# One of sixteen one-hot comparisons per group moved from VectorE to GpSimd

## The reference, cut to what matters

```python
x = _layernorm(x + _L0_gnn_ref(x, edge_index, ...))   # GIN: S = segment_sum(X[src], dst), 4 times
x = _layernorm(x + _L1_gnn_ref(x, edge_attr_64, edge_index, ...))   # edge MLP
x = _layernorm(x + _L2_gnn_ref(x, edge_index, ...))   # segment softmax, 3 times
x = _layernorm(x + _L3_gnn_ref(x, edge_attr_20, src, dst, edge_weight, ...))   # filtered interaction
```

## Time and profile before

| what | value |
|---|---|
| median of three runs | 2368.28 us |
| the profiled execution | 2367.29 us |
| span of the profiled execution, first to last instruction | 2365.6 us |
| mean granted TensorE clock | 0.788 of full speed |
| `adjacency`, first to last instruction | about 103.8 to 302.4 us of the span |
| of these, VectorE without a gap | 107 to 295 us |

### The profile page before, as it was taken

The page is one execution under the profiler, slowest core; times in us unless marked ns, Lnnn a source line. Parts: engine busy times, 40 slices in busy tenths (PEclk is TensorE's granted clock), DMA queues, the critical chain, the costliest instruction groups (busy, mean ns, idle before and its releaser), DMA issues. The chain is left out here.

```text
span 2365.6 us, 43422 instructions
## 1 busy us (share of the span) xinstructions
PE 1890.2 (80%) x8323; PEld 1345.6 (57%) x8323; DVE 1520.9 (64%) x4653; ACT 916.0 (39%) x2112; POOL 1368.3 (58%) x1338
## 2 busy tenths in 40 slices
PE   3488868878799998999879989989974676667676
PEld 1266654554688888888655545545553554555554
DVE  7899921112477776777546666586556777777775
ACT  1399901111112222222136055074034666666663
POOL 2300057776277777777518727637706777777770
PEclk9999978888755555555579999999986778777777
DMA  0000021111244444444411101101132222222220
GB/s 11 4 0 0 0 56 17 17 17 16 78 119 117 118 119 117 120 118 117 114 32 17 18 9 18 16 11 17 18 120 73 64 64 65 64 65 65 65 64 35
DMA packets 197096, 128.57 MB, mean 54 GB/s; under 512 B 138144, under 2 KB 179993, under 8 KB 195872
## 3 DMA queue, kind: packets, MB, share of 16 engines
q0 software_dynamic: 40256, 60.21, 11.9%
q1 hardware_dynamic: 151820, 59.71, 10.1%
q10 hardware_dynamic: 4822, 6.56, 0.8%
HBM read 106.83 MB, written 13.34 MB: 51 GB/s over the span
## 5 line engine op out<-in xcount | busy, mean ns | idle before, releaser
L2112 POOL DMA_INDIRECT adj<-h_rows,adj x416 | 396.7, 953 | 136.6 <-issue 79.6
L1193 POOL DMA_INDIRECT work<-p_rows,small x416 | 397.0, 954 | 128.0 <-issue 102.2
L1554 POOL DMA_INDIRECT edge_rows<-pay,small x249 | 305.7, 1228 | 75.5 <-issue 74.3
L2289 PE MATMUL ps<-adj 128*128 128x125 f32 x928 | 208.5, 362 | 162.5 <-DVE work L2190 160.0
L2289 PEld LDWEIGHTS ps<-adj 128*128 128x128 f32 x928 | 171.8, 255 | 258.1 <-issue 161.2
L1360 PE MATMUL ps<-work 128*128 x1024 | 300.2, 448 | 19.4 <-DVE work L1251 17.8
L1371 PE MATMUL ps<-small,work 128*128 128x64 f32 x1024 | 253.4, 402 | 37.2 <-issue 36.1
L1312 ACT ACTIVATE work<-work 128x256 f32<-128x256 f32 x256 | 106.6, 416 | 438.4 <-DVE work L1270 424.6
L1371 PEld LDWEIGHTS ps<-small,work 128*128 128x128 f32 x1024 | 241.7, 325 | 58.2 <-issue 57.0
L1360 PEld LDWEIGHTS ps<-work 128*128 128x128 f32 x1024 | 237.9, 321 | 28.6 <-issue 26.5
L697 POOL DMA_INDIRECT edge_rows<-pay,small x176 | 210.3, 1195 | 64.1 <-issue 61.7
(11 more groups left out here) (358 smaller groups left out, 3036.7 us busy)
## 6 DMA issues: line engine op xcount, KB each, us to landing
work<-dst_all SPq DMA_DIRECT2D x256, 64.0 KB
work<-edge_attr SPq DMA_DIRECT2D x256, 64.0 KB
edge_rows<-pay,small POOLq DMA_INDIRECT x425, 2.7
work<-p_rows,small POOLq DMA_INDIRECT x416
adj<-h_rows,adj POOLq DMA_INDIRECT x416
adj<-adj SPq DMA_DIRECT2D x232, 24.0 KB
pay<-edge_pay SPq DMA_DIRECT2D x106, 46.9 KB
work<-x_kept SPq DMA_DIRECT2D x2, 1562.5 KB, 6.4
```

The lines of the kernel that those rows point to most:

```text
L1193: eng.indirect_dma_start(gathered[:, at:at + D], None, p_rows[:, :], bass.IndirectOffsetOnAxis(ap=src_i[:, c:c + 1], axis=0)).then_inc(s_g ...
L1554: eng.indirect_dma_start(edge_rows[:, :], bass.IndirectOffsetOnAxis(ap=place[:, k:k + 1], axis=0), pay[:, k * ROW:(k + 1) * ROW], None).th ...
L2112: eng.indirect_dma_start(gathered[:, at:at + D], None, h_rows[:, :], bass.IndirectOffsetOnAxis(ap=row3_i[:, c, DST_C:DST_C + 1], axis=0)). ...
L2289: ins = eng.matmul(SUM[v % 2], msg[b][:, k * D:(k + 1) * D], hot[b][:, k * P:(k + 1) * P], start=k == 0, stop=k == PAIR - 1)
```

## The change

In each full group the one-hot with v = 3 of window k = 1 is made by GpSimd in place of VectorE, with the same instruction (`tensor_scalar`, `is_equal`, int16 in, bf16 out, 500 columns) into the same buffer. VectorE skips it, `hots_before` and the count of VectorE's one-hots per group (`GD`, 14 before, 13 after) leave it out, and TensorE waits for GpSimd's own semaphore there and for VectorE's count up to the one before. GpSimd waits, as VectorE does, until the buffer's last reader is done. Its loop is written out over the 39 groups that have a window k = 1.

```diff
     BY_ACT = [0, 2]
-    GA, GD = len(BY_ACT), WG * F - len(BY_ACT)
+    BY_POOL = 1
+    GA, GD = len(BY_ACT), WG * F - len(BY_ACT) - 1
+    s_pool = sem("hots_by_gpsimd")
...
+    def by_pool(k, v):
+        return v == F - 1 and k == BY_POOL
+
     def hots_before(k, v):
-        return sum(1 for j in range(WG) for u in range(F) if (j, u) < (k, v) and not by_act(j, u))
+        return sum(1 for j in range(WG) for u in range(F) if (j, u) < (k, v) and not by_act(j, u) and not by_pool(j, u))
...
@@ gpsimd, after the constants
+            eng.wait_ge(s_const, 4)
+
+            for g in range(NG):
+                if g * WG + BY_POOL < NW:
+                    eng.wait_ge(s_used, g * GV + BY_POOL * F + F)
+                    at = g * WG + BY_POOL + (F - 1) * NW
+                    eng.tensor_scalar(ring[BY_POOL][F - 1], code, key_v[:, at:at + 1], None,
+                                      ALU.is_equal).then_inc(s_pool, 1)
...
@@ vector
-                        if by_act(k, v):
+                        if by_act(k, v) or by_pool(k, v):
                             continue
...
@@ tensor
                             eng.wait_ge(s_near, g * GA + (BY_ACT.index(k) + 1))
+                            eng.wait_ge(s_code, g * GD + hots_before(k, v))
+                        elif by_pool(k, v):
+                            eng.wait_ge(s_pool, g + 1)
                             eng.wait_ge(s_code, g * GD + hots_before(k, v))
```

## The result

The changed kernel takes 2388.37 us (median of five runs, 2383.3 to 2389.92) against 2368.28 (now five runs as well, 2366.31 to 2372.66): a ratio of 1.0076, 95% interval 1.0063 to 1.0089. It is slower, by 15 to 21 us. The forecast was 2382, with a range of 2366 to 2403.

The account below looks back on a forecast made before the run. VectorE was taken to bound the adjacency stage at 4.81 us a group, ScalarE close at 4.75. Losing 0.26 and adding X - 0.15 (X = 0.76) gave +13.7 us over 39 groups: 2368.3 + 13.7 = 2382.0, range 2366 to 2403.

Parts of the forecast that it names:

- Removed: In adjacency, VectorE loses 39 comparisons of 0.26 us, 10.1 us; alone the stage shrinks only 2.2, ScalarE becoming the bound.
- The duration X: Time of GpSimd's 500-column comparison in adjacency, taken as 0.76 us from its other instructions, ends 0.55 and 1.27.
- The stall, X - 0.15: In adjacency, one VectorE instruction a group is stopped for GpSimd's whole comparison less 0.15 us, on the shared SBUF way.
- The sign given for it: In the changed profile, one line 498 (or 490) instance a group is longer, near 365 ns + X - 0.15; median unchanged.
- The sum, +13.7: Over adjacency's 39 groups: each group 4.81 - 0.26 + (X - 0.15) = 5.16 us, 0.35 more than before.
- Line 498 is of the kind that is stopped: VectorE's comparison in adjacency, a fast form reading and writing SBUF, was expected to stop while GpSimd works.
- Half groups of 2.41 and 2.75: In adjacency, half groups would alternate, one near 2.41 us and one near 2.75.
- A: Rival: no stall in adjacency, ScalarE becomes the bound, stage shrinks 2.2 us, kernel 2366.1; chance 0.14.
- B (starved): Rival: GpSimd gets in only when VectorE stands still in adjacency; +1.1 us a group, +43, kernel 2411; chance 0.05.
- C: Rival: GpSimd first loads code for the comparison, first one-hot about 5 us late once, kernel 2387; chance 0.04.

## Why the prediction was right, and by what

- *Removed: 10.1 us of VectorE, of which only 2.2 could become time.* Right: 2.3 measured, and 9.7 where VectorE stays the bound. This was the most solid step, and it rested on ScalarE's own beat, not on its busy share.
- *The duration X of GpSimd's comparison, 0.76, ends 0.55 and 1.27.* Wrong, and outside the bounds: 1.52 alone, 1.74 to 1.77 in most groups. None of the neighbours in the earlier trace rows is a `tensor_scalar`, and at 500 columns this operation is dearer than even the two-input addition (1.52 against 1.18 us). The dearest neighbour should not have been taken as a ceiling. The estimates from the Trainium skill (GPSIMD Engine Reference), 0.43 and 0.85 us before fixed costs, were too low as well: beside VectorE three instructions of 250 columns took 2.87 us and three of 500 took 4.75, so 500 columns without the fixed part are some 1.25 us. The dearer of the two rates stands in section 7 of that page.
- *The stall, X - 0.15 for one VectorE instruction.* Wrong for this operation: two stops, 0.67 together. It was drawn from the earlier trace rows, a memset and additions; one stop is also what a copy, an iota and an addition make when priced by themselves, though 0.08 to 0.16 us shorter than by the rule. Beside the comparison VectorE runs at full speed in the middle; nothing in the trace before shows that. The sign given for it failed with it: not one long instruction a group of up to 0.98 us, but two of at most 0.69 (the pair comparison was hit only twice), and the median went from 361 to 339 ns.
- *The sum, +13.7.* It came out by luck. The two errors cancel: 0.61 forecast for the stall, 0.67 measured, so +0.41 a group in place of +0.35 and +16.5 for the stage. With the true X my rule would have given 1.52 - 0.15 - 0.26 = 1.11 a group, +43 us, outside the range. The forecast of the time is right and its middle steps, duration and stall, are not. What held is the inequality, that VectorE loses more than 0.26 a group.
- *Line 498 is of the kind that is stopped.* Right, and the contrast with forms that read PSUM, seen in one scan, is confirmed (7.84 and 7.84 us). The rule of the Trainium skill (SBUF — State Buffer, "Who interferes with whom") that the first to come holds the pair for its whole instruction would stop VectorE for 1.5 us each time; in this trace VectorE ran a full-speed instruction at 184.78 in the middle of GpSimd's, and the loss was 0.67.
- *Half groups of 2.41 and 2.75.* Wrong: 2.15 and 3.08 us. The comparison is saved in the first half, and GpSimd, released by the product that ends window 1, works in the second.
- *The rivals.* A is refuted: the stops are there. B (starved) doesn't show as a cost, though two of GpSimd's instructions took 3.58 and 3.66 us; nobody waited. C is refuted: GpSimd's first comparison came at 106.65, at once behind its last iota.
- The median moved 20.1, the stage 16.5. The difference is inside the interval of 15 to 21 us, and in the profiled pair most of it is the layer norm above, where TensorE's granted clock differed and the change touches nothing.

## What to carry to other kernels

Price the transfer of elementwise work from VectorE to GpSimd by what it takes back: in this stage a 500-column `tensor_scalar` cost VectorE 0.67 us when GpSimd did it and 0.26 us when VectorE did it itself, so no slack in the dependences could make it pay while VectorE is the bound. Beside VectorE instructions that read PSUM it was free. For much smaller pieces the question is open: at 125 columns GpSimd's instruction took back only 0.13 us, and the one comparison of 125 columns that VectorE makes in this stage (line 508) was followed by the next after 0.21 us; no run moved such a piece. Before moving work off the bound engine, take the beat of the next one from its starts in a stretch without waits: here it capped any gain at 2.3 us of 10. And when an operation is not in the trace, its neighbours don't bound it from above.

## What the runs showed of the hardware that was not expected

- A GpSimd `tensor_scalar` of 500 columns takes 1.50 to 1.53 us for every type and for both operations tried (comparing and adding), against 0.57 (1.70 / 3) for a copy.
- It stops VectorE's fast comparison twice, for 0.34 us each at 500 columns in the stage, and in between one instruction of VectorE's runs at full speed (three of them at 1000 columns). A copy or an iota stops it once, for 0.35 to 0.38 us, a two-input addition once for 0.87.
- The pair comparison (two inputs in SBUF) is stopped once by GpSimd's comparison (0.40 us), and makes that longer (6.86 us for three, in place of 4.55); VectorE's float32 comparison does so too (5.92), its fast one hardly (4.75). That one of the two spells is GpSimd's reading and the other its writing fits this and the iota's single stop; it was not tested directly, and the copy, which reads and writes, makes only one stop.
